# Three groups of indirect transfers on 127 partitions instead of 128, in a two-layer graph kernel

## The reference, cut to what matters

```python
N, E, D = 12500, 412500, 32            # nodes, edges sorted by dst, features
h = relu(layernorm(x))
# layer 0: attention over incoming edges
e = leaky(s_src[src] + s_dst[dst]); m = segment_max(e, dst); ex = exp(e - m[dst])
x = x + segment_sum(h[src] * (ex / segment_sum(ex, dst)[dst])[:, None], dst)
h = relu(layernorm(x))
# layer 1: relation-dependent messages; 86 relations, 16 bases
msg = einsum('eb,ebo->eo', w_comp[etype], einsum('ei,bio->ebo', h[src], weight))
a = relu(tanh(sum(x_hat[e] * y_hat[e]) / sqrt(D)))   # x_hat from h[src], y_hat from h[dst] and etype
nei = segment_sum(a[:, None] * msg, dst)
x = x + relu(nei + h[src[last_edge_of_each_dst]] @ self_loop_weight)
```

## Time and profile before

| | |
|---|---|
| Median of 2 runs | 8989.97 us (8989.13 to 8990.8) |
| Span of the profiled execution | 9951.8 us |
| POOL busy in it | 7332.1 us, 6,953 instructions |
| DVE, ACT, PE busy | 4014.6, 1271.4, 349.8 us |

### The profile page before, as it was taken

One profiled execution on the slowest core, in us unless ns is written; L12 is line 12 of the kernel. 1 busy time (PEld: TensorE's weight loads), 2 busy tenths in 40 slices (PEclk: granted clock), 3 DMA queues, 4 the chain that ended last, 5 costly groups with the idle time before them and its releaser, 6 DMA issues.

```text
span 9951.8 us, 26480 instructions
## 1 busy us (share of the span) xinstructions
PE 349.8 (4%) x1742; PEld 162.6 (2%) x1742; DVE 4014.6 (40%) x4037; ACT 1271.4 (13%) x2008; POOL 7332.1 (74%) x6953
## 2 busy tenths in 40 slices
PE   0000000000000000000371000000000000000000
PEld 0000000000000000000130000000000000000000
DVE  5621011111100111111355666666666666666663
ACT  0010000000000000000362111111111111111110
POOL 6677777777777777777546777777777777777776
PEclk9999999999999999999986555555555555555555
DMA  3321111111111111111499888888888888888883
GB/s 80 106 68 34 42 42 42 42 42 42 33 41 42 42 42 42 42 40 33 177 403 309 259 250 256 251 253 253 252 253 251 254 251 252 254 251 252 253 253 106
DMA packets 527258, 1540.17 MB, mean 155 GB/s; under 512 B 175478, under 2 KB 243811, under 8 KB 506612
## 3 DMA queue, kind: packets, MB, share of 16 engines
q0 software_dynamic: 381664, 1066.15, 39.7%
q1 hardware_dynamic: 145555, 473.62, 12.5%
HBM read 1130.40 MB, written 407.74 MB: 155 GB/s over the span
## 4 chain that ended last, share of the span: by engine, by line
POOL 68%; issue 24%; DVE 3%; DMA 2%; another core or an unknown queue 1%; PE 1%; POOLq 0%; ACT 0%; SPq 0%; DVEq 0%; ACTq 0%
POOL arena L592 67%; DMA layer_rows<-arena 2%; DVE ps L984 1%; POOL dst_score_at_starts L627 1%; PE ps L873 0%; PE ps L874 0%; POOLq L627 0%; DVE arena L1145 0%; DVE arena L1187 0%; DVE arena L1127 0%; DMA last_dst_of_block<-dst_float 0%; DMA attention_weights<-in_L_gnn_attn_w 0%; DVE arena L962 0%; POOLq L677 0%
## 5 line engine op out<-in xcount | busy, mean ns | idle before, releaser
L592 POOL DMA_INDIRECT arena<-layer_rows,edge_row_index x6448 | 6845.0, 1062 | 2172.5 <-issue 2123.5
L1187 DVE COPY_PREDICATED arena<-ps,arena 128x6144 f32<-128x6144 uint32 (+3 forms) x540 | 1821.2, 3373 | 41.8
L1057 DVE TENSOR_TENSOR arena<-arena,ps 128x62 f32<-128x62 f32 x52 | 13.9, 267 | 3405.5 <-DMA arena<-layer_rows,edge_row_index 3405.5
L727 ACT ACTIVATE ps<-arena 128x62 f32<-128x62 f32 x52 | 11.8, 226 | 3543.4 <-issue 3535.6
L1180 DVE TENSOR_TENSOR h_nodes<-arena,ps 128x384 f32<-128x384 f32 x135 | 74.5, 552 | 942.5 <-DMA arena<-layer_rows,edge_row_index 728.0
L1170 DVE TENSOR_TENSOR_SCAN ps<-weights_and_zeros,ps 128x800 f32<-128x800 f32 x135 | 245.7, 1820 | 493.6 <-issue 394.6
L795 ACT ACTIVATE weights_and_zeros<-same_dst_as_before 128x768 f32 (+1 forms) x135 | 113.3, 839 | 2146.7 <-issue 1713.9
L665 POOL DMA_INDIRECT y_hat_at_starts<-aggregate_nodes,start_index x98 | 99.1, 1011 | 229.5 <-ACT aggregate_nodes L775 133.5
L1195 DVE TENSOR_TENSOR_SCAN weights_and_zeros<-weights_and_zeros,ps 128x800 f32<-128x800 f32 x135 | 244.6, 1812 | 4.7
L735 ACT ACTIVATE arena<-arena 128x2046 f32<-128x2046 f32 x52 | 198.7, 3820 | 341.4 <-issue 216.6
L803 ACT ACTIVATE ps<-arena 128x24 f32<-128x24 f32 x135 | 26.1, 194 | 1667.7 <-issue 1508.3
(11 more groups left out here) (199 smaller groups left out, 2251.1 us busy)
## 6 DMA issues: line engine op xcount, KB each, us to landing
layer_rows<-arena SPq DMA_DIRECT2D x98, 1616.0 KB
arena<-layer_rows,edge_row_index POOLq DMA_INDIRECT x6448
layer_scans<-weights_and_zeros SPq DMA_DIRECT2D x134, 768.0 KB
layer_scans<-arena SPq DMA_DIRECT2D x52, 1054.0 KB
y_hat_at_starts<-weights_and_zeros SPq DMA_DIRECT2D x52, 992.0 KB
weights_and_zeros<-y_hat_at_starts SPq DMA_DIRECT2D x134, 384.0 KB
layer_rows<-weights_and_zeros SPq DMA_DIRECT2D x49, 320.0 KB
edge_row_index<-row_of_edge SPq DMA_DIRECT2D x134, 12.0 KB
```

Of the source, the lines that this page charges most:

```text
L592: pool.indirect_dma_start(tile, None, table, bass.IndirectOffsetOnAxis(ap=index, axis=0)) \
L1187: done(v.copy_predicated(rows[:, :, M1:M1 + half], spread(bits[i][:, 0:k], [P, k, half]), rows[:, :, M1 + half:M1 + 2 * half]))
```

## The change

A helper `held(j)` gives 127 from node column 54 on and 128 before it. The score scatter, the y_hat scatter and the gather of layer 1's sums take that many partitions of their index and data tiles. It touches 44 of the 98 instructions of each of the three sets, 132 in all; the last partition of `sums1` is then left unwritten from column 54 on. The number and the order of the instructions are the same on every engine.

```diff
         @block.gpsimd
         def _(pool):
+            def held(j):
+                return whole if j >= n_rest else P
+
...
             def score_at_start(j):
-                pool.indirect_dma_start(z0_d, bass.IndirectOffsetOnAxis(ap=scat[:, j:j + 1], axis=0),
-                                        small[:, j:j + 1], None, bounds_check=EP - 1, oob_is_err=False) \
+                pool.indirect_dma_start(z0_d, bass.IndirectOffsetOnAxis(ap=scat[0:held(j), j:j + 1], axis=0),
+                                        small[0:held(j), j:j + 1], None, bounds_check=EP - 1, oob_is_err=False) \
                     .then_inc(s_z0_d, 16)
...
                 pool.wait_ge(s_ev_act, 6 * j + 12)
-                pool.indirect_dma_start(z1_d, bass.IndirectOffsetOnAxis(ap=scat[:, j:j + 1], axis=0),
-                                        yhat[:, j, :], None, bounds_check=EP - 1, oob_is_err=False) \
+                pool.indirect_dma_start(z1_d, bass.IndirectOffsetOnAxis(ap=scat[0:held(j), j:j + 1], axis=0),
+                                        yhat[0:held(j), j, :], None, bounds_check=EP - 1, oob_is_err=False) \
                     .then_inc(s_z1_d, 16)
...
             for j in range(J):
-                gather(sums1[:, j, :], r1_d, last[:, j:j + 1], s_agg1[j // JQ])
+                gather(sums1[0:held(j), j, :], r1_d, last[0:held(j), j:j + 1], s_agg1[j // JQ])
```

## The result

The changed kernel takes 9235.22 us (2 runs, 9233.57 to 9236.87) against 8989.97 us: ratio 1.0272, 95% interval 1.0256 to 1.0289, so 245 us or 2.7% slower.

A forecast was written before the change was run, and what follows sets the result against it. POOL was taken as the bound, busy 7332.1 us of 9951.8. Score scatter 44 x 0, y_hat scatter 0 (covered), sums 44 x 0 - 0.6 gave -0.6 us on 8990, so 8989 us; range 8960 to 9450 us.

The forecast's parts named there:

- rival 2: Score scatter and sums mainly: POOL makes 127-row transfers row by row, 2.9 us more each, 9258 us; chance 0.33 above 2%.
- I take x = 0: All three touched sets: x, POOL's extra time for a 127-row transfer over a 128-row one, is zero.
- rival 1: DMA engines: each 127-row transfer goes to one engine, POOL as before; +3 to +125 us; chance 0.13, shared with small POOL cost.
- Covered by 115 us of idle time: y_hat scatter: POOL waits for ACT, idle 2.6 us for each of 44, so extra POOL time below that adds 0.
- POOL's stream passes its cost on in full: Score scatter and sums: POOL issues unbroken, so 44 times the extra cost per transfer reaches the end in each.
- a gain over 2% is excluded: Score scatter and sums: even DMAs costing POOL nothing would save only 88 x 1.25 = 110 us, 1.2%.
- the landing of the score scatter is covered: Score scatter: later landing goes unnoticed, as POOL first asks for DVE's result some 27 us after it is ready.
- the last landing of the sums grows: End of the sums' gather: with one engine for each transfer, the last landing is later by 2.7 us.
- differences in the profile overstate those of the median: Whole kernel: profiled span lies 961.8 us above the runs' median; its differences, taken as the median's, overstate only a little.

The follow-up runs named there:

- the delay: Kernel before with all 128 rows, POOL clearing unused memory four times (2.35 us) after each y_hat scatter from column 54 on: 9960.86 us, ratio 1.0006.

## Why the prediction was wrong

I forecast no change, 8989 us, with 0.66 on "same", and measured are 9235 us, 2.7% more. That lies in the range, which reached up to 9450 us for rival 2's sake, and near that rival's 9258 us, which had 0.33.

- **The step that failed is "I take x = 0".** I took the price of a 127-row transfer from the 128-row transfer with one row dropped, as the nearest row. A dropped row leaves the shape alone, and the shape is what is paid for: x is 1.6 us of POOL plus 0.5 us of stall (some 20 us in 44 transfers), about 2.1 us. The rule that the Trainium skill states told the shape's effect on the engines used; I let it bear on the engines alone (rival 1). That the same split can set the steps in which POOL makes the entries I did ask, in rival 2, but the sum left it out, as no row had a transfer with another count.
- **Rival 2's mechanism was right and its step too long.** A step is 0.0134 us, where I took 0.024 between bounds of 0.005 and 0.118, so x came out as 2.9 us instead of 1.6; the stalls, which it did not have, brought back 0.5 us of that. For score scatter and sums it had 88 x 2.9 = 255 us, and measured are 88 + 91 = 179. For the y_hat scatter it had 13 us, and measured are 68. That its total came within 23 us is luck: the two errors nearly cancel.
- **"Covered by 115 us of idle time", the second term that failed, was nearly right of POOL and wrong of the stage.** POOL's time is covered but for some 7 us, as the delay showed. But the stage is bound by the DMA engines, and the transfer loads all of them, not one: 68 us in place of the 0 of the sum. Rival 1 had a load of one engine there, at most 53 us; its premise, that the other engines have nothing to do, was wrong.
- **Right:** that POOL's stream passes its cost on in full in the score scatter and the sums; that a gain over 2% is excluded; that the landing of the score scatter is covered; that the last landing of the sums grows, in rival 1 (by 4.0 us from the last start, of which 1.6 are POOL's; I had 2.7 without any of POOL's).
- **The reference.** My sentence that differences in the profile overstate those of the median took the chip's difference for that of profiling. It cost nothing in the sum, but it hid 20 us when the two profiles were first compared.

No version here beats the kernel before: 126 or fewer partitions leave nodes out, and even with 16 partitions a transfer costs POOL 0.846 us of the 0.945.

## What to carry to other kernels

What an indirect DMA costs POOL here goes by the number of steps, partitions divided by their largest divisor up to 16, and not by bytes: leave the unused partition in, and in a scatter let an index out of bounds drop its row. When a change turns an even shape into a prime one, price the shape itself; a row of the trace with the old shape says nothing about it. And a transfer that POOL's idle time covers is not free in a stage that the DMA engines bound.

## What the runs showed of the hardware that I had not expected

- A transfer whose rows go to one engine makes work for the 15 others as well: in the sums 143 packets instead of 32, and 15.7 us of engine time instead of 2.8.
- POOL stands still for about 4 us after every seventh 127-row transfer, for nearly 10 us where the DMA engines are full, and not at all with 122 or 124 rows.
- The same kernel takes 8990 us on one chip and 9955 us on another; the main gathers' 0.945 us become 1.062 there, while the gathers of the sums keep their median of 0.945.
- A scatter that alternates with a gather takes 1.02 us, one after another of its kind 0.98 us (y_hat stage).
